# A cross-attention and mixture-of-experts layer on one core: the steps around the routing in a new order, pauses at every third scatter, and expert scatters sent singly at first

## The chip, the cores and the metric

The kernel runs on one core of a Trainium2 chip. Its time is the device time of one execution in microseconds (us); the runs shown are given by their median. A profile is one further execution, recorded by the hardware profiler, with its span in the same unit. Engines are called PE (TensorE), DVE (VectorE), ACT (ScalarE), POOL (GpSimd) and SP (SyncE).

## What is computed

`x` is 16 blocks of 128 tokens with 128 features, `ctx` has the same shape. The reference, cut to what matters:

```
def xattn(Q, K, V):                       # Q = layernorm(x), K = V = ctx, 16 heads of 8 features each
    Q_ = Q.reshape(B, L, 16, 8) @ Wq + bq # and K_, V_ in the same way, 64 wide
    scores = einsum('blhk,blgk->blhg', Q_, K_) / sqrt(64)   # per token: heads against heads
    y = einsum('blhg,blgv->blhv', softmax(scores), V_)
    return y.reshape(B, L, 1024) @ Wo + bo

def ffn(x):                               # 8 experts, top 2 of them per token, 2048 tokens
    probs = softmax(x @ router_w)
    expert_gate, expert_index = top_k(probs, 2)
    v = x @ (wv * sv)[e]
    y = gelu(x @ (w * s)[e])
    out = (v * y) @ (w1 * s1)[e]          # for both chosen experts e
    return sum(expert_gate * out)

x = x + xattn(layernorm(x), ctx, ctx)
x = x + ffn(layernorm(x))
```

## The kernel before

Everything is written out by hand: each engine has a program of its own, and semaphores join them. There are two stages that overlap in the middle.

**Attention.** 16 tiles of 128 tokens (NT = 16) go through a software pipeline in groups of four (G = 4, four groups NG, numbered 0 to 3). The `step(g, j)` of an engine issues what that engine does in one step for several tiles at once: `tile_at(g, j, lag)` gives the tile that is `lag` stages behind. The steps of the loop `STEADY` end with tile 15 entering the scores; what is left is written out behind the loop, engine by engine ("the end" below). For a tile t:

- ACT writes the first layernorm `xn` (L600), PE turns it (L844) and multiplies.
- DVE forms the products `qk` (L1114, 128x2048), PE sums them (L856), ACT copies `scoresT` (L610), PE finishes the scores (L865, L878).
- DVE: `maximum` (L1146, L1150); ACT: `exponentials` (L669); DVE: `normalise` (L1164 to L1168), which leaves `probs`.
- `values` (L318) multiplies probabilities with the context for a range of the 16 keys: POOL does the first 11 (`POOL_KEYS`) and DVE, as `value_share`, the last 5. For the last tile, 15, POOL does 6 (`LAST_POOL_KEYS`) and DVE 10. PE sums the products in `value_sum` (L899), ACT copies `zT` (`z_turned`, L650), PE makes the output in `output_sum` (L907 to L909), ACT copies it to `x_sb` (`residual`, L655).

**Routing.** When the four tiles of a group n are through, the group is normalised a second time and routed. DVE: `second_statistics` of each tile (L1174, L1177). POOL: `second_rstd` (L493 to L499), four small operations. ACT: `normed` (L678), four activations. PE: `second_turn` (L916); ACT: `turned` (L685); PE: `router_product` (L926). DVE: `choices` (L1187 to L1203), PE: `places` (L936 to L939), ACT: `logits_exponentials` (L701), DVE: `positions` (L1213 to L1228), ACT: `rows_but_gates` (L695, L696) and `gates_in` (L661). Then POOL scatters the group's rows to `routed` in DRAM with eight indirect DMAs of 128 rows (`scatters`, L540). Groups 0 and 1 send theirs without any wait, in portions that `sends(n)` lays between the steps of the loop. Groups 2 and 3 wait before every even scatter but the first until all earlier ones of the group have landed:

```
for m in range(first, end):
    if n >= EARLY_G and m and m % 2 == 0:
        pool.wait_ge(scattered[n], 16 * m)
    pool.indirect_dma_start(
```

The last group is split: `second_rstd` and `normed` are called for its first three tiles and then for the fourth. ACT's exponential and its GELU need different tables; `load_gelu` (L590) loads the latter early, and L701 carries a load of the former where it stands behind a GELU.

**Expert tiles.** The routed rows, sorted by expert, are 39 tiles of 128 rows (TILES = 39), numbered 0 to 38. Tiles 0 to 8 (EARLY = 9) hold rows of groups 0 and 1 alone and may start when these have landed; tiles 9 to 38 wait for all four groups. SP loads a tile into one of 12 buffers `xs` (XB = 12, L389), PE turns it (`turn_rows`, L961), ACT copies `xsT` (`rows_turned`, L718) and the gate weights `g_tile` (`gate_weights`, L713), DVE the value weights `v_tile` (L1308); PE does `products` (L976), ACT `gelu` (L725), DVE `hidden` (L1316), PE `down` (L995), DVE `gated` (L1325), which writes `yo`. POOL scatters `yo` to `expert_out` with one indirect DMA per tile (L561); before every even tile it waits until the scatter of the tile before has landed. SP loads tile t + 12 only when `y_sent` says that the scatter of tile t has landed, since it takes its buffer. `turn_rows` of a tile stands on PE ahead of `products` of the tile before it. Every engine takes its program in order; PE's `products(1, 1)` waits for `residual` of attention tile 15 (`x2_ready`), whose bank it uses.

**The last part.** When every expert scatter has landed (SP, L420), SP gathers `expert_out` in five pieces (L424), DVE adds the pairs and the residual (L1378, L1381), and SP stores (L427).

## Time and profile before

| | |
|---|---|
| median of 3 runs | 280.63 us (280.06 to 281.09) |
| the profiled execution | 278.34 us |
| its span | 276.6 us |
| PE busy | 237.7 us (86% of the span) |
| DVE busy | 178.0 us (64%) |
| POOL busy | 151.9 us (55%) |
| ACT busy | 118.5 us (43%) |
| TensorE clock granted | 0.952 of full speed over the span |

The profiled execution lies 1.74 us above its span (what is around it) and 2.29 us below the median. Times of the trace count from the start of the span. The attention takes about the first 136 us, expert tiles run from there to 260 us, and the gather, the sums and the store take the rest. The profile gives, for each instruction, its start, its duration, and how long its engine had been idle before it with what ended that idle time; and it gives the chain of waits, which is the path of work followed back from the last instruction.

### The profile page before, as it was taken

The page shows a single profiled execution, that of the slowest core. Times are in us where ns is not written, and L with a number is a line of the kernel's source. Part 1 is how long each engine was busy: PE and PEld are TensorE (multiplying, and loading weights), DVE is VectorE, ACT ScalarE, POOL GpSimd, SP SyncE. Part 2 cuts the span into 40 slices and gives each one's busy share as a digit, 9 for nine tenths or more (in the row PEclk, how much of TensorE's full clock was granted, in tenths as well). Part 3 has the DMA queues.
Part 4 walks back from the last instruction along what each step waited for, and adds up shares of the span by engine and source line. Part 5 has one row for each costly group of instructions (what it writes and reads, how often), then busy time and mean ns, then how long its engine had stood idle before and what let it go on. Part 6 is the DMA issues. An engine that isn't in the chain of part 4 may idle for free.

```text
span 276.6 us, 6414 instructions
## 1 busy us (share of the span) xinstructions
PE 237.7 (86%) x1883; PEld 223.0 (81%) x1884; DVE 178.0 (64%) x475; ACT 118.5 (43%) x297; POOL 151.9 (55%) x160
## 2 busy tenths in 40 slices
PE   7997999979997999797996985999999999999500
PEld 7976888868886888696896974999999999999400
DVE  2799799877998789969174472454465455555216
ACT  2443422464544563326485242454465555554000
POOL 6956549754688859886545555253532423333300
PEclk9999999999999999979899899899999999999955
DMA  5979999995000100001200112312221121000058
GB/s 143 301 186 419 294 315 382 378 380 197 1 19 17 34 11 22 29 31 40 59 31 29 49 32 67 79 57 52 59 58 34 53 55 39 28 10 26 3 181 274
DMA packets 25518, 30.94 MB, mean 112 GB/s; under 512 B 2652, under 2 KB 16896, under 8 KB 25362
## 3 DMA queue, kind: packets, MB, share of 16 engines
q1 hardware_dynamic: 21708, 25.28, 29.1%
q0 software_dynamic: 2528, 4.77, 5.5%
q10 hardware_dynamic: 1254, 0.55, 0.7%
q8 instruction: 14, 0.23, 0.3%
q14 instruction: 14, 0.11, 0.1%
HBM read 16.26 MB, written 14.79 MB: 112 GB/s over the span
## 4 chain that ended last, share of the span: by engine, by line
PE 63%; DVE 11%; DMA 10%; POOL 5%; issue 5%; ACT 4%; SPq 1%; POOLq 0%; ACTq 0%; DVEq 0%
PE bank L976 20%; PE bank L995 10%; PE bank L899 9%; PE bank L856 8%; DMA routed<-rows,pos 6%; DVE qk L1114 3%; PE bank L783 3%; POOL routed L540 3%; DMA pv<-expert_out 2%; POOL pv L318 2%; PE bank L865 2%; ACT xn L600 2%; PE bank L907 2%; PE bank L909 2%; PE bank L908 2%
## 5 line engine op out<-in xcount | busy, mean ns | idle before, releaser
L561 POOL DMA_INDIRECT expert_out<-yo,xs x39 | 38.1, 978 | 59.1 <-DVE yo L1325 36.3
L318 POOL TENSOR_TENSOR pv<-probs,ctx_sb 128x1408 f32<-128x1408 f32 (+1 forms) x16 | 45.9, 2868 | 21.8 <-DVE probs L1168 18.9
L1316 DVE TENSOR_TENSOR hid<-bank,act_sb 128x512 f32<-128x512 f32 x39 | 26.9, 690 | 30.7 <-PE bank L976 16.0
L540 POOL DMA_INDIRECT routed<-rows,pos x32 | 35.0, 1093 | 21.1 <-DMA routed<-rows,pos 9.8
L995 PE MATMUL bank<-w_sb,hid 128*128 x312 | 43.1, 283 | 2.5 <-DVE yo L1325 2.4
L976 PE MATMUL bank<-xsT,g_tile 128*128 128x128 f32 x312 | 42.6, 280 | 1.1 <-issue 1.1
L995 PEld LDWEIGHTS bank<-w_sb,hid 128*128 128x128 f32 x312 | 39.4, 198 | 3.1 <-issue 3.1
L976 PE MATMUL bank<-xsT,v_tile 128*128 128x128 f32 x312 | 41.8, 277 | 0.0
L976 PEld LDWEIGHTS bank<-xsT,g_tile 128*128 128x128 f32 x312 | 39.1, 197 | 1.4 <-issue 1.3
L976 PEld LDWEIGHTS bank<-xsT,v_tile 128*128 128x128 f32 x312 | 38.5, 194 | 0.0
L1114 DVE TENSOR_TENSOR qk<-bank,ctx_ig 128x2048 f32<-128x2048 f32 x16 | 36.5, 2285 | 2.3 <-ACT ctx_ig L585 1.9
L856 PE MATMUL bank<-ident,qk 128*128 128x128 f32 x256 | 32.1, 281 | 2.6 <-DVE qk L1114 2.6
L899 PE MATMUL bank<-ident,pv 128*128 128x128 f32 x256 | 32.2, 281 | 1.6 <-POOL pv L318 1.6
L725 ACT ACTIVATE act_sb<-bank 128x512 f32<-128x512 f32 x39 | 23.3, 597 | 22.6 <-PE bank L976 19.8
L899 PEld LDWEIGHTS bank<-ident,pv 128*128 128x128 f32 x256 | 30.2, 146 | 3.3 <-issue 2.2
L713 ACT COPY g_tile<-g_sb 128x512 f32 x39 | 24.1, 618 | 19.0 <-PE bank L976 14.7
L856 PEld LDWEIGHTS bank<-ident,qk 128*128 128x128 f32 x256 | 29.6, 145 | 3.0 <-issue 3.0
L1308 DVE COPY v_tile<-v_sb 128x512 f32 x39 | 17.1, 438 | 18.2 <-issue 16.9
L1325 DVE SCALAR_TENSOR_TENSOR yo<-bank,xs,wo_sb 128x128 f32<-128x128 f32 x39 | 13.7, 351 | 11.2 <-PE bank L995 8.8
L318 DVE TENSOR_TENSOR pv<-probs,ctx_sb 128x640 f32<-128x640 f32 (+1 forms) x16 | 20.4, 1276 | 0.1
L718 ACT COPY xsT<-bank 128x128 f32<-128x128 f32 x39 | 10.3, 264 | 17.5 <-PE bank L961 17.3
L610 ACT COPY scoresT<-bank 128x256 f32<-128x256 f32 x16 | 6.0, 373 | 27.2 <-PE bank L856 24.3
(171 smaller groups left out, 330.0 us busy)
## 6 DMA issues: line engine op xcount, KB each, us to landing
routed<-pad_rows SPq DMA_DIRECT2D x4, 2080.0 KB, 20.5
xs<-routed SPq DMA_DIRECT2D x39, 65.0 KB
g_sb<-in_L_ffn_w_dram SPq DMA_DIRECT2D x1, 2048.0 KB, 11.7
g_scale<-in_L_ffn_s_dram SPq DMA_DIRECT2D x1, 2048.0 KB, 16.3
v_sb<-in_L_ffn_wv_dram SPq DMA_DIRECT2D x1, 2048.0 KB, 28.0
pv<-expert_out SPq DMA_DIRECT2D x3, 512.0 KB, 4.9
x_sb<-in_x_dram SPq DMA_DIRECT2D x4, 256.0 KB, 6.2
ctx_sb<-in_ctx_dram SPq DMA_DIRECT2D x4, 256.0 KB, 6.3
```

The lines of the kernel that those rows point to most:

```text
L318: return eng.tensor_tensor(pv[:, b, g0:g1, :, :], probs[:, b, :, g0:g1].rearrange("p h g -> p g h").unsqueeze(3).to_broadcast([P, many, H, ...
L540: pool.indirect_dma_start(out=routed[:, :], out_offset=bass.IndirectOffsetOnAxis(ap=pos[:, m % TOP, m // TOP:m // TOP + 1], axis=0), in_=r ...
L561: pool.indirect_dma_start(out=expert_out[:, :], out_offset=bass.IndirectOffsetOnAxis(ap=xs_i[:, t % XB, P:P + 1], axis=0), in_=yo[:, t % X ...
L713: nc.scalar.copy(g_tile[:, c % 2, :], g_sb[:, bass.ds(at, F)]).then_inc(g_tile_ready, 1)
L725: nc.scalar.activation(act_sb[:, c % 2, :], bank[1 + c % 2][:, :], ACT.Gelu_apprx_tanh).then_inc(act_ready, 1)
L856: mm = nc.tensor.matmul(part, qk[:, b, i, c * P:(c + 1) * P], ident[:, :], start=(i == 0), stop=(i == HD - 1), is_transpose=True)
L899: mm = nc.tensor.matmul(bank[4][:, 0:P], pv[:, t % 2, key, :, :].rearrange("p h i -> p (h i)"), ident[:, :], start=(key == 0), stop=(key = ...
L976: mm = nc.tensor.matmul(psum[:, n * P:n * P + P], weights[:, c % 2, n * P:n * P + P], xsT[:, c % 2, :], start=True, stop=True)
L995: mm = nc.tensor.matmul(y_bank(t, c)[:, 0:P], hid[:, c % 2, n * P:n * P + P], w1_sb[:, bass.ds(y_at + n * P, P)], start=(n == 0), stop=(n ...
L1114: v.tensor_tensor(qk[:, b, :, :].rearrange("p i (h g) -> p i h g", h=H), q_bank(b)[:, 0:P].rearrange("p (i h) -> p i h", i=HD).unsqueeze(3 ...
L1308: v.tensor_copy(v_tile[:, c % 2, :], v_sb[:, bass.ds(at, F)]).then_inc(v_tile_ready, 1)
L1316: v.tensor_tensor(hid[:, c % 2, :], bank[3 + c % 2][:, :], act_sb[:, c % 2, :], ALU.mult).then_inc(hid_ready, 1)
```

## The change

Seven edits, by engine:

1. POOL, in the loop: `second_rstd` of a group stands behind `values` of its step, no longer ahead of it.
2. ACT, in the loop: `normed` moves from the end of a step into the next step, behind the exponentials and ahead of the copy of `scoresT`.
3. POOL: group 1 sends 3, 3 and 2 scatters between steps instead of 2, 3 and 3; groups 2 and 3 wait before every third scatter instead of every second; and a wait for all eight scatters of the group is added behind each of these groups.
4. POOL and DVE, at the end: POOL has no part of the values of tile 15, DVE does all 16 keys. POOL sends four scatters of group 2, not one, ahead of the last group's `second_rstd`.
5. POOL: expert scatters 1 to 11 wait each for the one before; scatters from 12 on wait for none.
6. ACT, PE, DVE, at the end: routing steps of group 2 go ahead of steps of tile 15 (`choices`, `places`, `logits_exponentials`, `gates_in`), `products(0, 0)` goes ahead of `value_sum(15)`, `normed` of the last group's first three tiles goes ahead of `residual(15)`, and `second_statistics(15)` goes behind `hidden(0, 0)`, the weights of tile 2 and `left_table`.
7. ACT: `gelu(2, 2)` goes ahead of the exponentials of the last group and of the two table loads.

```diff
-            return {9: 3, 10: 6, 11: G * TOP} if n < EARLY_G - 1 else {8: 2, 9: 5, 10: G * TOP}
+            return {9: 3, 10: 6, 11: G * TOP} if n < EARLY_G - 1 else {8: 3, 9: 6, 10: G * TOP}
...
+        IN_A_ROW = 3
@@ POOL, step @@
-                    if a := group_at(g, j, NORM):
-                        second_rstd(a[0])
                     a = tile_at(g, j, 1)
...
                         values(pool, t, b, 0, POOL_KEYS).then_inc(pv_pool, 1)
+                    if a := group_at(g, j, NORM):
+                        second_rstd(a[0])
@@ POOL, scatters @@
-                        if n >= EARLY_G and m and m % 2 == 0:
+                        if n >= EARLY_G and m and m % IN_A_ROW == 0:
                             pool.wait_ge(scattered[n], 16 * m)
@@ POOL, the end @@
-                pool.wait_ge(p_normed, NT)
-                pool.wait_ge(zT_psum, NT - 2)
-                values(pool, NT - 1, (NT - 1) % 2, 0, LAST_POOL_KEYS).then_inc(pv_pool, 1)
-                scatters(NG - 2, 0, 1)
+                scatters(NG - 2, 0, 4)
                 second_rstd(NG - 1, 0, G - 1, NG)
                 second_rstd(NG - 1, G - 1, G, NG + 1)
-                scatters(NG - 2, 1, G * TOP)
+                scatters(NG - 2, 4, G * TOP)
+                pool.wait_ge(scattered[NG - 2], SENT)
                 scatters(NG - 1, 0, G * TOP)
+                pool.wait_ge(scattered[NG - 1], SENT)

                 for t in range(TILES):
                     pool.wait_ge(yo_ready, t + 1)
-                    if t and t % 2 == 0:
-                        pool.wait_ge(y_sent[(t - 1) % XB], 16 * ((t - 1) // XB + 1))
+                    if 0 < t < XB:
+                        pool.wait_ge(y_sent[t - 1], 16)
@@ ACT, step @@
                     if a := tile_at(g, j, 1):
                         exponentials(a[0])
+                    if a := group_at(g, j, LOGITS):
+                        normed(a[0])
...
-                    if a := group_at(g, j, NORM):
-                        normed(a[0])
@@ PE, value_sum @@
-                    pe.wait_ge(pv_pool, t + 1)
+                    if t < NT - 1:
+                        pe.wait_ge(pv_pool, t + 1)
@@ ACT, the end @@
-                exponentials(NT - 1)
                 logits_exponentials(NG - 2)
                 gate_weights(0, 0)
+                exponentials(NT - 1)
                 z_turned(NT - 2)
                 rows_but_gates(NG - 2)
+                gates_in(NG - 2)
                 residual(NT - 2)
                 rows_turned(0, 0)
                 load_gelu()
-                gates_in(NG - 2)
+                gelu(0, 0)
+                gate_weights(1, 1)
                 z_turned(NT - 1)
-                gate_weights(1, 1)
+                rows_turned(1, 1)
+                normed(NG - 1, 0, G - 1, NG)
                 residual(NT - 1)
-                rows_turned(1, 1)
-                gelu(0, 0)
-                normed(NG - 1, 0, G - 1, NG)
-                normed(NG - 1, G - 1, G, NG + 1)
                 gate_weights(2, 2)
                 gelu(1, 1)
+                normed(NG - 1, G - 1, G, NG + 1)
+                turned(NG - 1)
                 rows_turned(2, 2)
-                turned(NG - 1)
                 gate_weights(3, 3)
+                rows_but_gates(NG - 1)
                 rows_turned(3, 3)
-                rows_but_gates(NG - 1)
+                gelu(2, 2)
                 logits_exponentials(NG - 1)
                 load_gelu()
-                gelu(2, 2)
                 gates_in(NG - 1)
@@ PE, the end @@
+                places(NG - 2)
                 value_sum(NT - 2)
-                places(NG - 2)
                 output_sum(NT - 2)
                 turn_rows(0, 0, 0)
+                products(0, 0)
                 value_sum(NT - 1)
                 turn_rows(1, 1, 0)
                 output_sum(NT - 1)
-                products(0, 0)
                 products(1, 1)
@@ DVE, the end @@
                 value_share(NT - 2)
                 value_weights(0, 0)
+                choices(NG - 2)
                 maximum(NT - 1)
-                choices(NG - 2)
                 normalise(NT - 1)
-                value_share(NT - 1, LAST_POOL_KEYS)
                 positions(NG - 2)
+                value_share(NT - 1, 0)
                 second_statistics(NT - 3)
                 second_statistics(NT - 2)
                 value_weights(1, 1)
-                second_statistics(NT - 1)
                 hidden(0, 0)
                 value_weights(2, 2)
                 left_table()
+                second_statistics(NT - 1)
                 hidden(1, 1)
```

Three places where instructions change their order. First POOL, from the step that normalises group 2 (`vtmp2` to `shift2`) to the end of the attention; `pv` are the values, `routed` the scatters.

```order
+L317 TENSOR_TENSOR pv<-probs,ctx_sb 128x1408
 L493 TENSOR_TENSOR vtmp2<-mv2,eps 128x4
 L495 TENSOR_TENSOR rstd2<-vtmp2,minus_half 128x4
 L496 TENSOR_TENSOR centre2<-mv2,minus_one 128x4
 L499 TENSOR_TENSOR shift2<-centre2,rstd2 128x4
-L318 TENSOR_TENSOR pv<-probs,ctx_sb 128x1408
-L540 DMA routed<-rows0,pos0 18432x130 x3
-L318 TENSOR_TENSOR pv<-probs,ctx_sb 128x1408
-L318 TENSOR_TENSOR pv<-probs,ctx_sb 128x768
-L540 DMA routed<-rows0,pos0 18432x130
+L540 DMA routed<-rows0,pos0 18432x130 x2
+L317 TENSOR_TENSOR pv<-probs,ctx_sb 128x1408
+L540 DMA routed<-rows0,pos0 18432x130 x4
```

The values of tile 13 now stand ahead of the four small operations, the 128x768 values of tile 15 are gone, and group 2's first four scatters stand together behind the values of tile 14.

Second ACT at the same place in the loop, from `z_turned` of tile 12: before,

```order
L650 COPY zT<-bank 128x128
L655 COPY x_sb<-bank 128x128
L678 ACTIVATE xn<-x_sb,shift,rstd 128x128 x4
L669 ACTIVATE probs<-shifted 128x256
L610 COPY scoresT<-bank 128x256
```

and with the change:

```order
L649 COPY zT<-bank 128x128
L654 COPY x_sb<-bank 128x128
L668 ACTIVATE probs<-shifted 128x256
L677 ACTIVATE xn<-x_sb,shift,rstd 128x128 x4
L611 COPY scoresT<-bank 128x256
```

The four activations of `normed` have moved behind the exponentials; in the steps of groups 0 and 1 the first layernorm's `xn` (L600) stands between the first two of these rows and the exponentials, so it is passed too.

Third ACT at the end, from `load_gelu` on. Before,

```order
L590 ACTIVATE pause_act<-eps 128x1
L661 COPY rows0<-gates0 128x8
L650 COPY zT<-bank4 128x128
L710 TENSOR_LOAD w_off
L710 ISA x2
L713 ISA
L713 COPY g_tile<-g_sb 128x512
L655 COPY x_sb<-bank4 128x128
L718 COPY xsT<-bank0 128x128
L725 ACTIVATE act_sb<-bank1 128x512
L678 ACTIVATE xn2<-x_sb,shift2,rstd2 128x128 x4
```

and with the change:

```order
L589 ACTIVATE pause_act<-eps 128x1
L724 ACTIVATE act_sb<-bank1 128x512
L709 TENSOR_LOAD w_off
L709 ISA x2
L712 ISA
L712 COPY g_tile<-g_sb 128x512
L649 COPY zT<-bank4 128x128
L717 COPY xsT<-bank0 128x128
L677 ACTIVATE xn2<-x_sb,shift2,rstd2 128x128 x3
L654 COPY x_sb<-bank4 128x128
```

The copy of the gates has left this stretch for a place ahead of the table load, and the copy of tile 15's output to `x_sb` stands behind three activations that need POOL's `shift2`.

## Rows read from the trace of the kernel before

**Rows 1.** Timeline, 55 to 58 us: ACT, then PE's next row. Start, duration, engine, instruction, [idle before].

```profile
55.56 1.65 ACT L678 ACTIVATE xn<-x_sb,shift,rstd 128x128 f32<-128x128 f32 x4
57.11 0.48 ACT L600 ACTIVATE xn<-x_sb,shift,rstd 128x128 f32<-128x128 f32 x1
...
57.64 0.33 PE L844 MATMUL bank<-ident,xn 128*128 128x128 f32 x1 [1.84 <-ACT xn L600]
```

**Rows 2.** Timeline, 78 to 88 us: DVE's share of the values twice, and POOL's.

```profile
78.51 0.81 DVE L318 TENSOR_TENSOR pv<-probs,ctx_sb 128x640 f32<-128x640 f32 x1
...
85.03 3.26 DVE L318 TENSOR_TENSOR pv<-probs,ctx_sb 128x640 f32<-128x640 f32 x1
...
84.77 2.84 POOL L318 TENSOR_TENSOR pv<-probs,ctx_sb 128x1408 f32<-128x1408 f32 x1
```

**Rows 3.** Timeline, 114 to 121 us: DVE's products of tile 15, and PE's sum of them.

```profile
114.38 2.29 DVE L1114 TENSOR_TENSOR qk<-bank,ctx_ig 128x2048 f32<-128x2048 f32 x1
...
116.81 3.44 PE L856 MATMUL bank<-ident,qk 128*128 128x128 f32 x16 [1.50 <-DVE qk L1114]
```

**Rows 4.** Timeline, 127 to 136 us: DVE, POOL and ACT, where the attention ends.

```profile
127.92 1.49 DVE L318 TENSOR_TENSOR pv<-probs,ctx_sb 128x1280 f32<-128x1280 f32 x1
...
127.97 2.94 POOL L318 TENSOR_TENSOR pv<-probs,ctx_sb 128x768 f32<-128x768 f32 x1 [2.26 <-DVE probs L1168]
132.87 1.02 POOL L540 DMA_INDIRECT routed<-rows,pos  x1 [1.96 <-ACT rows L661]
134.20 0.88 POOL L495 TENSOR_TENSOR rstd<-vtmp,minus_half 128x3 f32<-128x3 f32 x1
...
131.81 0.19 ACT L661 COPY rows<-gates 128x8 f32<-128x8 f32 x1
```

**Rows 5.** Timeline, POOL, 138 to 166 us: scatters 1 and 2 of group 2, then 0, 2 and 7 of group 3.

```profile
138.86 1.19 POOL L540 DMA_INDIRECT routed<-rows,pos  x1 [0.51 <-issue]
141.63 0.97 POOL L540 DMA_INDIRECT routed<-rows,pos  x1 [1.58 <-DMA routed<-rows,pos]
...
151.87 1.05 POOL L540 DMA_INDIRECT routed<-rows,pos  x1 [0.30 <-issue]
...
155.80 0.97 POOL L540 DMA_INDIRECT routed<-rows,pos  x1 [1.60 <-DMA routed<-rows,pos]
...
164.98 0.97 POOL L540 DMA_INDIRECT routed<-rows,pos  x1 [0.30 <-issue]
```

**Rows 6.** Timeline, ACT, 143 to 150 us: a table load, and the copy of the last group's gates.

```profile
145.32 1.28 ACT L590 ACT_TABLE_LOAD   x1
146.61 0.20 ACT L590 ACTIVATE pause_act<-eps 128x1 f32<-128x1 f32 x1
...
149.60 0.20 ACT L661 COPY rows<-gates 128x8 f32<-128x8 f32 x1 [2.30 <-DVE gates L1226]
```

**Rows 7.** Chain of waits, 164 to 175 us: start, duration, what.

```profile
164.98 2.39 DMA routed<-rows,pos
...
168.67 1.44 DMA xs<-routed
...
170.49 2.46 PE bank L976 x16
```

**Rows 8.** Timeline, PE: the turn of expert tile 9, and that of tile 23.

```profile
170.16 0.33 PE L961 MATMUL bank<-ident,xs 128*128 128x128 f32 x1 [3.33 <-DMA xs<-routed]
...
211.01 0.27 PE L961 MATMUL bank<-ident,xs 128*128 128x128 f32 x1
```

**Rows 9.** Timeline, POOL: expert scatters 2, 6 and 38; then DVE's last `yo`.

```profile
170.59 0.97 POOL L561 DMA_INDIRECT expert_out<-yo,xs  x1 [2.10 <-DMA expert_out<-yo,xs]
...
180.50 0.97 POOL L561 DMA_INDIRECT expert_out<-yo,xs  x1 [3.30 <-DMA expert_out<-yo,xs]
...
262.26 0.97 POOL L561 DMA_INDIRECT expert_out<-yo,xs  x1 [2.05 <-DMA expert_out<-yo,xs]
...
259.74 0.35 DVE L1325 SCALAR_TENSOR_TENSOR yo<-bank,xs,wo_sb 128x128 f32<-128x128 f32 x1 [0.77 <-PE bank L995]
```

1 line of the change is left out of this document (removed).

## The prediction

> **What bounds the kernel now.** I read the chain of waits first, then the timeline of each engine where the chain changes hands. Up to 107 us the chain runs on PE, with short pieces of ACT. At the boundary of a group it carries an extra piece: ACT does the four activations of `normed` from 55.56 to 57.11 us, only then the `xn` of the next tile, and PE has been idle for 1.84 us when that arrives [rows 1]; it recurs at 86 us. Then DVE takes over: PE waits 1.50 us for `qk` of tile 15 [rows 3]. At the end of the attention the chain goes through POOL's values of tile 15, which run beside DVE's and end at 130.9 us; POOL's scatter 0 of group 2 starts at 132.87, behind ACT's copy of the gates [rows 4]. From 138.86 to 164.98 us the chain is POOL and the landing of its scatters [rows 5]; the last one lands after 2.39 us, SP loads expert tile 9 at 168.67 [rows 7], and PE, idle for 3.33 us, goes on at 170.16 [rows 8]. From there PE runs at 2.79 us per expert tile until 258.5 us. So what counts is when PE can turn tile 9, and what follows the last `yo`: scatter 38 waits until 262.26 us, though its input was done at 260.09 [rows 9].
>
> **The change, part by part.** Edit by edit, in the order of time.
>
> *`normed` behind `xn` (edits 1 and 2).* At group 0 `xn` starts 57.11 - 55.56 = 1.55 us earlier [rows 1]. `normed` then runs beside PE's sum over `qk`, and POOL's `shift2` is ready for it although `values` now precedes it. At group 1 POOL has three scatters ahead of both, so `shift2` comes after another 2.84 us of values [rows 2]; I lay `normed` out to end some 0.7 us after PE wants its results for `second_turn`. Gain 1.55 + 0.85 = 2.4 us. Bounds for the two together: 0.6 us (both late) and 3.1 us (none).
>
> *Three scatters of group 1 instead of two (edit 3).* The third puts POOL's values of tile 12 back by 1.27 us (0.97 + 0.30) [rows 5]. DVE's share takes 0.81 us alone and 3.26 us where it starts 0.26 us behind POOL's 2.84 us: it gets done only when POOL is through [rows 2]. The share of tile 12 meets POOL's values, so DVE, which by then sets the pace [rows 3], loses some 1.2 us. Bounds: nothing (it had slack) and 2.45 us, the whole of 3.26 - 0.81. The Trainium skill, "GPSIMD Engine Reference", Key points, says that GpSimd shares its SBUF interfaces with VectorE, contention being with VectorE instructions in a 2-port mode or with two SBUF inputs. The trace agrees, and the same rule speaks for edit 4, where DVE's last share runs with POOL idle. Left after these: 1.2 us at tile 15.
>
> *The end of the attention (edits 4 and 6).* With `choices(2)` ahead of `maximum(15)` and `places(2)` ahead of `value_sum(14)`, DVE finishes `positions(2)` near 128.1 us. ACT copies the gates ahead of the table load at 128.85, 2.95 us earlier than at 131.81, so scatter 0 of group 2 moves from 132.87 to 129.9 [rows 4]. DVE's 16 keys cost 2.29 us, the row of the same size [rows 3], and end at 130.4 us, before PE wants them. POOL then goes scatters 0 to 3: 1.27 + 1.27 + 2.57 (0.97 and a wait of 1.60) + 0.97 = 6.1, to 136.0 [rows 5]; `second_rstd` of three tiles some 1.7 us around its 0.88 us power [rows 4], to 137.7. Here is the **new wait**: ACT stands at `normed` of these tiles with `residual(15)` behind it. `normed` takes 1.25 us (three quarters of 1.65 [rows 1]), `residual` and DVE's statistics 0.85, POOL's last `second_rstd` 1.35: done at 141.2 us instead of 138.35 (138.86 less 0.51 [rows 5]), 2.85 us later. PE's `products(1, 1)` wait for the same residual until 139.3, idle for over 4 us, and go on at a lower clock; PE has about 4 us to spare before tile 9, so this costs nothing as long as that lasts.
>
> *Group 2's last scatters and the last group's routing (edits 3, 6, 7).* Scatters 4 to 7 start at 141.7, 143.0, 145.5 and 146.8; with the added wait for all eight, POOL is free at 149.4. The routing of group 3 begins 2.85 us late, but `gelu(2, 2)` no longer stands behind two table loads of 1.28 us each [rows 6], so that `hidden(2, 2)` and `positions(3)` follow at once. I get the exponentials' end at 148.7, `positions` at 149.9 and, behind the GELU table load, the gates at 150.2, against 149.60 [rows 6]. The first scatter of group 3 then starts 1.06 us after the copy, as at group 2 [rows 4]: 151.25, against 151.87 [rows 5], so 0.6 us earlier. Bounds: 149.4 (POOL alone, 2.45 us earlier) and 153.9 (150.2 + 1.06 and another 2.6 us, one turn of a waited scatter).
>
> *Every third instead of every second.* From scatter 0 to 7 of group 3 it is 164.98 - 151.87 = 13.1 us now, with three waits [rows 5]. With two waits it is 5 x 1.27 + 2 x 2.6 = 11.6 us. That holds if three in flight land as fast as two; scatters behind another one land no later than single ones (2.39 us [rows 7]), so I take the full 1.5 us; bounds 0 and 1.5. The last scatter starts at 162.9 instead of 165.0, and tile 9 is turned 2.1 us earlier, near 168.1.
>
> *Expert scatters (edit 5).* A waited one takes 0.97 + 2.10 = 3.07 us [rows 9]. The first can go when group 3 has landed, at 165.5; scatters 1 to 11 in single file put scatter 11 at 165.5 + 11 x 3.07 = 199.3, and with one long one of 4.27 us (0.97 + 3.30 [rows 9]) at 200.5. Its landing (2.7) and SP's load (2.7, from 167.4 to 170.1 [rows 7, 8]) make tile 23 ready at 205.9. PE turns tile 23 at 211.01 now [rows 8] and at 208.9 with the gain: 3 us to spare. Behind scatter 11 POOL sends one each 1.27 us and has caught up by tile 24 or so. Cost nothing; when the cover is gone PE waits one for one. At the tail the wait of scatter 38 goes: it starts 1.27 us behind scatter 37, which goes at 259.24, so at 260.5 instead of 262.26. Gain 1.75 us.
>
> **Sum.** -2.1 (tile 9) - 1.75 (tail) = -3.85 us. The profiled execution would go from 278.34 to 274.5; it lies 2.3 us below the median of 280.63, so I forecast 276.8 us for the median. What a measurement here can tell from no change is 0.5%, 1.4 us. The forecast case spans -5.6 to -2.
>
> **Rivals.**
> - *The routing of the last group eats the scatters' gain* (15 in 100). For it: the new wait on ACT, and PE running slow behind its idle time: 16 transposes took 3.44 us after 1.50 us idle [rows 3], and `products` 2.46 after 3.33 us [rows 7]. Against it: 0.6 us of room on that path before it is even with now, and 1.5 from the waits behind it. With 2.1 us more delay only the tail is left: 280.63 - 1.75 = 278.9; with 3.5 more, 280.3.
> - *Slower: the buffers starve* (10 in 100). The place is expert scatters 1 to 11. Now a pair takes 1.27 + 3.07, or 2.17 us per tile, under PE's 2.79; single file takes 3.07, above it. It decides where the mean of the eleven passes 3.07 + (4.2 / 11) = 3.45 us, which uses up the room. If all were of the long kind, 4.27 us, they would take 11 x 1.2 = 13.2 us more, less 4.2 of room: PE loses 9.0 us, and the kernel takes 276.8 + 9.0 = 285.8 us. For it: long waits exist [rows 9]. Against it: most are near 3.07.
> - *More than forecast* (7 in 100). `gates_in` of group 3 in time for POOL alone, 149.4: another 1.85 us, 275.0.
> - *Table loads cost twice what their row says* (3 in 100). Then the last gates come behind two further stretches of 1.3 us: the gain at tile 9 is gone, with 0.5 us lost, and the tail leaves 279.4. Against it: 1.28 us load from 145.32, and the next activation starts at 146.61 [rows 6]. The Trainium skill, "ScalarE: Activation LUTs", What ACT_TABLE_LOAD costs, gives about 1.28 us for the load and about 1.38 for a drain, 2.66 in all; the row shows the first alone.
> - *The change does nothing* is within the first: the waits and the order are on the engines' queues as written.
>
> **How the numbers follow.** Forecast case 65, rivals 15, 10, 7 and 3 in 100. Faster by over 0.5% (under 279.2): 65 + 7 and half of the first rival, 0.79. Within 0.5%: the rest of it and the fourth, 0.11. Slower: 0.10. The range reaches from the third rival, with some of the front bounds, at 274.4, to the first and fourth, at 279.8; the slower rival is left outside.
>
> **What would show it right or wrong.** In the new profile: no ACT `xn` behind four activations at 55 and 86 us, tile 15's `qk` about 1 us earlier; group 2's first scatter near 130; ACT idle before `normed` until 137.7 and PE idle before tile 1's products over 4 us; eight scatters of group 3 in 11.6 us from 151.2; tile 9 turned near 168.1; expert scatters 3.07 us apart until 200 us and no PE wait for a load between 180 and 212; last scatter at the last `yo`. Wrong it would be if tile 9 is turned after 170, if three scatters in a row land later, or if PE waits for `xs` anywhere behind tile 9.

## The result, and the profile after

The changed kernel took 281.43 us (median of 4 runs, 281.18 to 283.07), beside 280.86 us (4 runs) for the kernel before in the same session. The ratio is 1.0138, with a 95% interval of 1.0077 to 1.0198. The same kernel run again on another chip (c_after, below) gave 1.0022 [0.9965, 1.0079]. The medians alone differ by 0.2%; a ratio compares only executions in the faster of the two states in which one kernel is found, so that here and below it need not equal the quotient of the medians. So the change is level to somewhat slower, and not the 1.4% faster of the forecast. Its profiled execution took 281.27 us.

The page of the changed kernel: span, busy time, granted clock in 40 slices of 7 us, and the chain by engine.

```profile
span 279.4 us, 6405 instructions
PE 240.2 (86%) x1883; PEld 223.7 (80%) x1884; DVE 183.6 (66%) x475; ACT 119.4 (43%) x297; POOL 148.9 (53%) x159
PEclk9999999999999999868589998799999999999965
PE 49%; DVE 18%; issue 10%; POOL 9%; DMA 8%; ACT 3%; SPq 1%; DVEq 1%; POOLq 0%; ACTq 0%
```

The same clock line of the kernel before:

```profile
PEclk9999999999999999979899899899999999999955
```

DVE is busy 5.6 us longer than before (183.6 against 178.0) with the same number of instructions; 0.8 us of that is work taken over from POOL (tile 15's values take 2.29 us instead of 1.49), the rest is instructions that take longer. The clock falls deeper and longer between 112 and 147 us, down to 0.5 of full speed in one slice. The timeline of the changed kernel, 112 to 127 us (start, duration, engine, instruction, [idle before and what ended it]), says where DVE's time went:

```profile
112.35 3.46 DVE L1247 TENSOR_SCALAR w_off<-tile_e 128x9 int32<-128x9 f32 x1
112.92 2.84 POOL L317 TENSOR_TENSOR pv<-probs,ctx_sb 128x1408 f32<-128x1408 f32 x1
116.66 2.29 DVE L1114 TENSOR_TENSOR qk<-bank,ctx_ig 128x2048 f32<-128x2048 f32 x1
119.10 3.65 PE L855 MATMUL bank<-ident,qk 128*128 128x128 f32 x16 [5.88 <-DVE qk L1114]
122.03 3.50 POOL L317 TENSOR_TENSOR pv<-probs,ctx_sb 128x1408 f32<-128x1408 f32 x1 [1.63 <-DVE probs L1168]
123.00 2.82 DVE L1308 COPY v_tile<-v_sb 128x512 f32 x1 [0.19 <-issue]
```

In the kernel before, the timeline of DVE has for the first of these:

```profile
113.12 0.17 DVE L1247 TENSOR_SCALAR w_off<-tile_e 128x9 int32<-128x9 f32 x1
```

An instruction on nine numbers per partition takes 3.46 us instead of 0.17: it ends at 115.81, just when POOL's values of tile 13 end (112.92 + 2.84 = 115.76). Then `qk` of tile 15, which was to come 1.2 us sooner than before, ends 2.3 us later, and PE waits 5.88 us for it instead of 1.50 [rows 3]. Its 16 matmuls then run at half the clock (3.65 us; 1.91 at full clock, for the tile before). They did so before the change too, for the most part (3.44 us [rows 3]). The copy of `v_tile` (0.43 us where POOL computes nothing) is held for 2.82 us in the same way.

The timeline of the changed kernel again, from the end of the attention to the last output: ACT, then POOL, PE and DVE.

```profile
134.12 0.20 ACT L660 COPY rows<-gates 128x8 f32<-128x8 f32 x1
...
143.21 1.26 ACT L677 ACTIVATE xn<-x_sb,shift,rstd 128x128 f32<-128x128 f32 x3 [0.38 <-POOL shift L499]
144.38 0.24 ACT L654 COPY x_sb<-bank 128x128 f32<-128x128 f32 x1
```

```profile
135.20 1.02 POOL L540 DMA_INDIRECT routed<-rows,pos  x1 [9.67 <-ACT rows L660]
...
156.45 0.97 POOL L540 DMA_INDIRECT routed<-rows,pos  x1 [1.67 <-DMA routed<-rows,pos]
...
162.58 0.97 POOL L540 DMA_INDIRECT routed<-rows,pos  x1 [2.61 <-DMA routed<-rows,pos]
...
168.96 0.97 POOL L540 DMA_INDIRECT routed<-rows,pos  x1 [0.30 <-issue]
...
265.04 0.97 POOL L560 DMA_INDIRECT expert_out<-yo,xs  x1 [0.30 <-DVE yo L1325]
```

```profile
174.28 0.48 PE L961 MATMUL bank<-ident,xs 128*128 128x128 f32 x1 [4.61 <-DMA xs<-routed]
...
215.54 0.27 PE L961 MATMUL bank<-ident,xs 128*128 128x128 f32 x1
...
264.33 0.35 DVE L1325 SCALAR_TENSOR_TENSOR yo<-bank,xs,wo_sb 128x128 f32<-128x128 f32 x1 [0.83 <-PE bank L995]
```

Against [rows 4, 5, 8, 9] the two profiles differ, stretch by stretch, by this much (after minus before). The milestones are the starts of the first `second_turn`, of the copy of group 2's gates, of the scatters, and of PE's turns of tiles 9 and 38, and the end of `qk` of tile 15 at 118.95 and 116.67 us:

| stretch | measured | forecast |
|---|---|---|
| start to `second_turn` of group 0 (57.45, 59.55) | -2.10 | -1.55 |
| to the end of `qk` of tile 15 | +4.38 | +0.35 |
| to the copy of group 2's gates | +0.03 | -1.75 |
| to the first scatter of group 3 | +2.27 | +2.35 |
| to its last scatter | -0.60 | -1.5 |
| to tile 9 turned | +0.14 | 0 |
| tile 9 to tile 38 (257.38, 252.84) | +0.42 | 0 |
| tile 38 to the last instruction | -1.75 | -1.75 |
| sum | +2.79 | -3.85 |

Of the difference of 6.6 us between sum and forecast, 4.0 us lie in one stretch, the one with the held `w_off` (3.29 us of it), and 1.8 in the next, in which the copy of `v_tile` is held.

### The profile page after: what moved, and what is told of

It reads as the page before. It is cut to its first block, busy times and chain, and to the rows that moved or that the text cites. A ratio compares the mean times of both kernels' runs of the same rounds, so it can differ in the third digit from the quotient of the medians.

```text
span 279.4 us, 6405 instructions
## 1 busy us (share of the span) xinstructions
PE 240.2 (86%) x1883; PEld 223.7 (80%) x1884; DVE 183.6 (66%) x475; ACT 119.4 (43%) x297; POOL 148.9 (53%) x159
## 4 chain that ended last, share of the span: by engine, by line
PE 49%; DVE 18%; issue 10%; POOL 9%; DMA 8%; ACT 3%; SPq 1%; DVEq 1%; POOLq 0%; ACTq 0%
PE bank L976 22%; PE bank L995 11%; PE bank L899 4%; POOL routed L540 4%; DVE qk L1114 4%; PE bank L855 4%; DMA routed<-rows,pos 3%; DVE pv L317 2%; DMA x_sb<-in_x_dram 2%; POOL pv L317 2%; DMA pv<-expert_out 2%; PE bank L961 1%; DVE w_off L1247 1%; DVE v_tile L1308 1%; ACT xn L599 1%
## 5 line engine op out<-in xcount | busy, mean ns | idle before, releaser
L317 POOL TENSOR_TENSOR pv<-probs,ctx_sb 128x1408 f32<-128x1408 f32 x15 | 43.6, 2907 | 20.3 <-DVE probs L1168 17.5
L540 POOL DMA_INDIRECT routed<-rows,pos x32 | 33.3, 1041 | 30.4 <-ACT rows L660 12.2
L976 PE MATMUL bank<-xsT,g_tile 128*128 128x128 f32 x312 | 43.4, 284 | 2.4 <-issue 1.1
L976 PE MATMUL bank<-xsT,v_tile 128*128 128x128 f32 x312 | 42.9, 282 | 0.0
L995 PE MATMUL bank<-w_sb,hid 128*128 x312 | 42.0, 278 | 0.2 <-DVE hid L1316 0.2
L976 PEld LDWEIGHTS bank<-xsT,v_tile 128*128 128x128 f32 x312 | 39.7, 199 | 0.0
L995 PEld LDWEIGHTS bank<-w_sb,hid 128*128 128x128 f32 x312 | 38.5, 194 | 0.7 <-issue 0.5
L1308 DVE COPY v_tile<-v_sb 128x512 f32 x39 | 20.0, 512 | 18.0 <-issue 17.7
L1325 DVE SCALAR_TENSOR_TENSOR yo<-bank,xs,wo_sb 128x128 f32<-128x128 f32 x39 | 13.7, 351 | 12.8 <-PE bank L995 11.4
L317 DVE TENSOR_TENSOR pv<-probs,ctx_sb 128x640 f32<-128x640 f32 (+1 forms) x16 | 18.9, 1184 | 0.0
## 6 DMA issues: line engine op xcount, KB each, us to landing
g_scale<-in_L_ffn_s_dram SPq DMA_DIRECT2D x1, 2048.0 KB, 15.3
```

The lines of the kernel that those rows point to most:

```text
L317: return eng.tensor_tensor(pv[:, b, g0:g1, :, :], probs[:, b, :, g0:g1].rearrange("p h g -> p g h").unsqueeze(3).to_broadcast([P, many, H, ...
L540: pool.indirect_dma_start(out=routed[:, :], out_offset=bass.IndirectOffsetOnAxis(ap=pos[:, m % TOP, m // TOP:m // TOP + 1], axis=0), in_=r ...
L976: mm = nc.tensor.matmul(psum[:, n * P:n * P + P], weights[:, c % 2, n * P:n * P + P], xsT[:, c % 2, :], start=True, stop=True)
L995: mm = nc.tensor.matmul(y_bank(t, c)[:, 0:P], hid[:, c % 2, n * P:n * P + P], w1_sb[:, bass.ds(y_at + n * P, P)], start=(n == 0), stop=(n ...
L1308: v.tensor_copy(v_tile[:, c % 2, :], v_sb[:, bass.ds(at, F)]).then_inc(v_tile_ready, 1)
```

## The experiments

The theory after the result (A): edit 1 puts POOL's values of tile 13 beside DVE's early expert table (a dozen small operations, `w_off` and `row_off` among them, that work out which expert each of the first nine tiles belongs to), and some of DVE's instructions stand until POOL is through. Rivals: the lower clock after a wait (C), the new order of the end (B), the single expert scatters (edit 5).

**Four kernels made from the change.** Line numbers shift by one or two in them.

a_wait_table: POOL's values of tile 13 wait for the table.

```diff
+                        if t == NT - 3:
+                            pool.wait_ge(early_ready, 1)
                         values(pool, t, b, 0, POOL_KEYS).then_inc(pv_pool, 1)
```

> The changed kernel, with one wait more: POOL's values of attention tile 13 wait until DVE has finished the early table. Theory A (a DVE instruction of the table, w_off at L1247, is held while POOL's values run: 3.46 us for a 128x9 operation that took 0.17 before the change): the row goes back to 0.17, qk of tile 15 ends 3.3 us earlier (near 115.6 instead of 118.95), PE's idle time before it falls from 5.9 to about 2.6 us, and the kernel takes about 4 us less than the changed one, near 277. Theory B (the long row is an effect of something else, and the loss comes from ACT standing at normed with tile 15's residual behind it): L1247 or the instructions behind it stay as long, and the time stays within 1 us of the changed kernel's 281.4.

a_rstd_first: edit 1 undone, `second_rstd` ahead of `values` in POOL's step.

```diff
+                    if a := group_at(g, j, NORM):
+                        second_rstd(a[0])
                     a = tile_at(g, j, 1)
...
-                    if a := group_at(g, j, NORM):
-                        second_rstd(a[0])
```

> The changed kernel with edit 1 alone undone: second_rstd stands ahead of POOL's values in its step again, so that the values of tile 13 start about 1.9 us later, near 114.8, behind the early table (which without a hold ends at 113.3). Theory A: L1247 takes 0.17 us, qk of tile 15 ends 3.3 us earlier, the hold moves to DVE's share of tile 13 (1.7 us for 0.8), and the time is 3 to 4 us under the changed kernel's. Theory B: no change beyond 1 us.

a_table_late: DVE builds the table behind `qk` of tile 15.

```diff
+                    if g * G + j == EARLY_TABLE + 2:
+                        early_table()
...
-                        early_table()
```

> The changed kernel with DVE's early table (12 small operations, about 3 us without a hold) behind qk of tile 15 instead of ahead of it. Theory A: qk of tile 15 ends at about 113, 6 us earlier (3.3 of hold and about 2.7 of the table's own time), PE waits for it hardly at all; the table itself then follows beside POOL's second_rstd and scatters and is not held, or costs 2 us of slack there. Time 5 to 6 us under the changed kernel's, near 276. Theory B: at most the table's own 2.7 us are won.

a_warm: PE does 24 filling matmuls before it waits for `qk` of tile 15.

```diff
+                        if t == NT - 1:
+                            fill(24)
                         pe.wait_ge(qk_ready, t + 1)
```

> The changed kernel with 24 products of the identity in front of PE's wait for qk of tile 15, which fill most of its 5.9 us of idle time; nothing else moves. This measures what the lower granted clock costs by itself (granted clock 0.67 in the stretch from 120 to 140). If the clock is a cost on the path: L855 of tile 15 takes 1.9 us instead of 3.65, the value sums of tiles 14 and 15 1.9 instead of 2.7, group 2's first scatter comes 2 us or more earlier, and the time falls by 2 to 3 us. If it is not: the granted clock rises, and the time stays within 0.7 us of 281.4.

Ratios to the kernel before: a_wait_table 1.0004 [0.9945, 1.0062], a_rstd_first 0.9997 [0.9944, 1.0050], a_table_late 1.0052 [1.0010, 1.0095], a_warm 1.0039 [0.9981, 1.0097]. The first three were each expected 3 to 6 us below the change's 281.4 us; their medians are 280.15, 278.36 and 280.20, that of the kernel before, run beside them, 279.90. The change itself was not run beside them. DVE's timeline of a_wait_table, then of a_rstd_first:

```profile
113.38 0.17 DVE L1249 TENSOR_SCALAR w_off<-tile_e 128x9 int32<-128x9 f32 x1
...
120.90 0.50 DVE L1310 COPY v_tile<-v_sb 128x512 f32 x1 [0.19 <-issue]
```

```profile
112.12 0.17 DVE L1247 TENSOR_SCALAR w_off<-tile_e 128x9 int32<-128x9 f32 x1
...
120.64 2.98 DVE L1308 COPY v_tile<-v_sb 128x512 f32 x1 [0.19 <-issue]
```

With POOL elsewhere the instruction is short again, and the stretch from the first `second_turn` to the end of `qk` of tile 15 falls from 61.5 us in the change to 58.4 and 57.4 (57.1 before). In the five profiles of kernels that have edit 1, and the table where it was, `w_off` takes 3.45 or 3.46 us (the change, c_after, a_warm, b_12, e_after_pairs); in the other thirteen it takes 0.17 or 0.18. So the hold, and edit 1 as its cause in this place, is shown. What it costs the whole kernel is not: both kernels only come level with the one before, and the change's own two ratios are 1.0138 and 1.0022, so that taking the hold out gave between 1.4% and nothing clear of noise.

In a_table_late `qk` of tile 15 ends earliest of all, 55.7 us after the first `second_turn`, and still nothing is gained. Its table meets POOL's values in the new place too (POOL's start at 114.47 and take 2.85 us), the copy of `v_tile` is held for 2.81 us, and the copy of group 2's gates comes 18.4 us behind `qk`, against 15.2 in the change. DVE's timeline of a_table_late:

```profile
114.57 0.21 DVE L1269 TENSOR_REDUCE n_tiles<-over 128x8 f32<-128x64 f32 x1
114.81 2.54 DVE L1270 TENSOR_SCALAR jump<-n_tiles 128x8 f32<-128x8 f32 x1
```

Of two small neighbours that both read and write SBUF, the reduction is not held and the TENSOR_SCALAR is.

In a_warm the matmuls run at full clock, and little comes of it, since DVE is held as before: the gates of group 2 come 14.8 us behind `qk` instead of 15.2. PE's timeline of a_warm:

```profile
119.86 1.97 PE L857 MATMUL bank<-ident,qk 128*128 128x128 f32 x16 [0.48 <-DVE qk L1116]
```

So the clock is worth at most 0.4 us here (C falls for this place), although PE itself needs 1.7 us less.

**The change again, and its halves.** c_after is the change itself. b_end keeps its end of the attention alone (edits 4, 6 and 7, and from edit 3 the pauses at every third scatter and the waits for all eight; edits 1, 2, 5 and the third scatter of group 1 undone). b_normed is the kernel before with edit 2 alone. d1 is b_normed with pauses at every third scatter, `gelu(2, 2)` ahead of the exponentials (edit 7), and no wait for expert scatters from tile 12 on.

```diff
# b_normed: ACT's step of the kernel before
                         exponentials(a[0])
+                    if a := group_at(g, j, LOGITS):
+                        normed(a[0])
...
-                    if a := group_at(g, j, NORM):
-                        normed(a[0])
# d1, on top of it
-                        if n >= EARLY_G and m and m % 2 == 0:
+                        if n >= EARLY_G and m and m % 3 == 0:
...
+                gelu(2, 2)
                 logits_exponentials(NG - 1)
                 load_gelu()
-                gelu(2, 2)
...
-                    if t and t % 2 == 0:
-                        pool.wait_ge(y_sent[(t - 1) % XB], 16 * ((t - 1) // XB + 1))
+                    if 0 < t < XB and t % 2 == 0:
+                        pool.wait_ge(y_sent[t - 1], 16)
```

> The changed kernel as it is, once more, as a control: run on the same chip and in the same rounds as the three beside it. Theory A and B both expect the trace of the first one: w_off at L1247 about 3.5 us, PE idle 5 to 6 us before the sum over qk of tile 15, and a time 0 to 1.5% above the kernel before.

> The loop of the kernel before (edits 1, 2, the order of group 1's scatters and edit 5 undone) with the end of the change: its new order on ACT, PE and DVE, tile 15's values on DVE alone, four scatters of group 2 first, waits at every third and behind each group. Theory A2 (beside the held instruction, the new end costs time itself: ACT stands at normed with tile 15's residual behind it, so the last group's shift2 comes late): counted from the first second_turn, the last shift2 comes 6 to 8 us later than in the kernel before (78.8 us there), the first scatter of group 3 2 to 3 us later, the turn of expert tile 9 1 to 1.5 us later; time 1 us over the kernel before. My prediction's theory (the new end is no loss, because the routing of the last group catches up): tile 9 is turned 2 us earlier than before.

> The kernel before with edit 2 alone: ACT's normed stands behind the exponentials of the next step, POOL's second_rstd stays ahead of the values. Expected if that edit is sound: the first two group boundaries are 1.5 us shorter each, POOL's values of tile 13 stay behind DVE's early table (both move by the same 3 us), no instruction of the table is held, and the kernel takes 2.5 to 3 us less than before, 277.5 where the kernel before takes 280.5. If the gain at the boundaries is always given back on DVE, whatever POOL does (the rival): qk of tile 15 ends where it did, within 0.7 us.

> The kernel before with edit 2, scatters of groups 2 and 3 waiting at every third (without the waits added behind each group), gelu(2, 2) ahead of the two table loads (edit 7), expert scatters in pairs up to tile 11 and without a wait from tile 12 on; POOL's order in the loop and the end of the attention stay as before. Theory A and A2: 3 us from the boundaries, 1.2 from group 2's scatters and 1.3 from group 3's, 1.75 at the tail: 6 to 7 us less than the kernel before, near 274. If the waits behind each group are needed for speed (scatters piling up land later), the 2.5 us of the scatters are missing: 276.5.

c_after 1.0022 [0.9965, 1.0079], b_end 1.0029 [0.9967, 1.0091], b_normed 0.9868 [0.9773, 0.9962], d1 0.9757 [0.9635, 0.9879]. Edit 2 alone is thus worth 1.3%, with an interval from 0.4 to 2.3%, about as much as the forecast gave the whole change (1.4%). Its profiled execution was one of its longest (279.97 us; median 278.30) and shows the gain only up to the end of `qk` of tile 15, 2.0 us earlier than before. The new end without the rest gains nothing: in b_end's profile (283.49 us, its longest execution) the first scatter of group 2 comes 14.9 us behind `qk` of tile 15 (16.2 before, 1.3 sooner), but the last shift of group 3 ends 26.9 us behind it (21.7 before). ACT's timeline of b_end:

```profile
145.22 1.26 ACT L677 ACTIVATE xn<-x_sb,shift,rstd 128x128 f32<-128x128 f32 x3 [4.38 <-POOL shift L499]
146.39 0.24 ACT L654 COPY x_sb<-bank 128x128 f32<-128x128 f32 x1
```

That is the wait of the forecast, ACT at `normed` behind POOL's four scatters with `residual(15)` behind it, and it costs 5.2 us at this point; the forecast laid out 2.85, which from tile 15's earlier end is 4.05. In d1, with the old end of the attention, the eight scatters of group 3 take 11.5 us (151.63 to 163.17), as forecast (11.6).

**Edit 1 by itself, a fill, the holds, and no pause.** b_12 is b_normed with edit 1. b_fill is the kernel before with 8 filling matmuls instead of one at each group's boundary. a_no_holds is a_rstd_first with `value_weights(0, 0)` behind `choices(2)` and `maximum(15)`, away from POOL's values. d2 is d1 without any pause in the scatters of groups 2 and 3.

```diff
# b_12: POOL's step, on top of b_normed
-                    if a := group_at(g, j, NORM):
-                        second_rstd(a[0])
...
                         values(pool, t, b, 0, POOL_KEYS).then_inc(pv_pool, 1)
+                    if a := group_at(g, j, NORM):
+                        second_rstd(a[0])
# b_fill
-                            fill(1)
+                            fill(8 if group_at(g, j, LOGITS) else 1)
# a_no_holds: DVE, on top of a_rstd_first
-                value_weights(0, 0)
                 choices(NG - 2)
                 maximum(NT - 1)
+                value_weights(0, 0)
# d2, on top of d1
-                        if n >= EARLY_G and m and m % 3 == 0:
-                            pool.wait_ge(scattered[n], 16 * m)
```

> The kernel before with edits 1 and 2: normed behind the exponentials and POOL's second_rstd behind the values. It differs from the run with edit 2 alone by POOL's order only. Theory A (a DVE instruction beside POOL's values is held): POOL's values of tile 13 start right behind its scatters, beside DVE's early table; one row of the table (w_off, s_off or jumps) takes 2.5 to 3.5 us instead of 0.2, qk of tile 15 ends 2.5 to 3 us later than with edit 2 alone (56.3 us behind the first second_turn there), and the 1.3% that edit 2 alone won is lost again. Without that mechanism the two are equal within 0.7 us.

> The kernel before with seven more products of the identity in PE's idle time of 1.84 us at the first two group boundaries; nothing else. Theory C: this idle time lies where the granted clock sometimes falls (in the profile of the run with the new end alone the sum over qk behind it took 3.62 us, in the profile of before 1.91), which is why runs of the kernel before spread from 277 to 282 us. Then these runs gather at the lower end, median 1 to 2 us under before, and the spread shrinks. If the clock has no part in the spread: median and spread as before, within 0.5 us.

> The changed kernel with second_rstd ahead of the values again (as the earlier run) and DVE's value weights of expert tile 0 behind choices and maximum, so that neither the early table nor that copy meets POOL's values. Theory A: the copy takes 0.43 us instead of 2.98, and group 2's first scatter starts 15 us behind the end of qk of tile 15 instead of 17.7; what is left of the loss is the new end's own (the last shift2 5 us later than before): time 2.5 to 4 us under before. If holds were not what mattered: as the run with second_rstd moved alone, level with before.

> The version with edit 2, edit 7 and no wait at the tail (d1), now with no wait at all between the scatters of groups 2 and 3. It tells whether scatters in a long row land later. If they do not: group 3's scatters take 7 x 1.27 = 8.9 us instead of 11.5, its first one comes at the gates, 1 to 2 us earlier, tile 9 is turned 3 to 4 us earlier unless PE itself arrives there first (it had 2.5 to 3 us to spare), and the kernel takes 2 to 3 us less than d1, 1.03 times faster than before or more. If they do: the last landing is more than 4 us behind the last issue, and the time is that of d1 within 1 us.

b_12 1.0035 [0.9984, 1.0086]: with edit 1 the gain of b_normed is not there. The two differ by POOL's order alone, but were run in different sessions; their intervals do not overlap. In the profiles the stretch from the first `second_turn` to the end of `qk` of tile 15 is 60.3 us against 56.3, and 3.3 us of that is the hold. DVE's and PE's timeline of b_12, then of b_normed:

```profile
111.94 3.46 DVE L1247 TENSOR_SCALAR w_off<-tile_e 128x9 int32<-128x9 f32 x1
...
118.69 3.65 PE L856 MATMUL bank<-ident,qk 128*128 128x128 f32 x16 [4.63 <-DVE qk L1114]
```

```profile
111.20 0.18 DVE L1247 TENSOR_SCALAR w_off<-tile_e 128x9 int32<-128x9 f32 x1
...
114.83 1.94 PE L856 MATMUL bank<-ident,qk 128*128 128x128 f32 x16 [1.25 <-DVE qk L1114]
```

b_fill 1.0103 [1.0027, 1.0179]: a miss. It was to keep PE's clock up at the boundaries and made the kernel slower; why is not shown. d2 1.0078 [1.0028, 1.0128]: a miss too, expected 2 to 3 us below d1. In its profile DVE is held again, by another instruction of the same table:

```profile
113.32 2.75 DVE L1270 SCALAR_TENSOR_TENSOR row_off<-tile_no,tile_row 128x9 int32<-128x9 f32 x1
```

and ACT stops twice: for 4.5 us until 147.87, in a row of seven scatters with no wait (140.62 to 148.50), and from 158.6 us for 7.6 us, in a row of ten (155.40 to 166.91). ACT's timeline of d2 ("remote" is a releaser that is none of the kernel's engines or transfers in view):

```profile
157.94 0.62 ACT L711 COPY g_tile<-g_sb 128x512 f32 x1
166.18 0.27 ACT L716 COPY xsT<-bank 128x128 f32<-128x128 f32 x1 [7.61 <-remote]
```

a_no_holds 1.0191 [1.0086, 1.0296], the greatest miss: `qk` of tile 15 ends at 115.1 us and the first scatter of group 2 starts at 130.95, 4.3 us ahead of the change, and yet the kernel is 1.9% slower. ACT's timeline of a_no_holds has the same stop, while POOL issues nine expert scatters in a row, 205.51 to 215.71:

```profile
207.70 0.62 ACT L712 COPY g_tile<-g_sb 128x512 f32 x1 [0.68 <-PE bank L976]
215.57 0.27 ACT L717 COPY xsT<-bank 128x128 f32<-128x128 f32 x1 [7.25 <-remote]
```

The turn of the tile had been on PE at 208.01, and so ACT had its input from 208.3 on. DVE stops as well, for 5.91 us until 214.23.

**Edit 5 by itself.** Four kernels follow up the stop of a_no_holds: e_nh_pairs and e_after_pairs are a_no_holds and the change with edit 5 undone, e_b_single is the kernel before with edit 5, e_d1_pairs is d1 with the waits of before between expert scatters.

```diff
# e_b_single; the other three have the lines of before here
-                    if t and t % 2 == 0:
-                        pool.wait_ge(y_sent[(t - 1) % XB], 16 * ((t - 1) // XB + 1))
+                    if 0 < t < XB:
+                        pool.wait_ge(y_sent[t - 1], 16)
```

> The run of the change without holds was 1.9% slower than before although the attention's end came early: in its trace ACT and DVE stand from 208 to 214-216 us while POOL issues nine expert scatters in a row with no wait between them (205.5 to 216.7), and PE loses some 5 us. Here the same kernel gets the waits of before between pairs of expert scatters (edit 5 undone, nothing else). If the long unwaited row is the cause: no idle time of over 2 us on ACT between 175 and 262 us, the ratio at 0.98 to 0.99. Rival, the loss has another cause (the chip, the clock): the ratio stays at 1.01 to 1.02.

> The change with edit 5 alone undone (waits between pairs of expert scatters as before). Theory, edit 5 costs on average some time by the stall behind unwaited scatters in some executions: 1 to 2 us faster than the change, ratio to before 0.995 to 1.000, and less scatter between executions. Rival, edit 5 gains (the tail's 1.75 us came from it): ratio 0.5% above the change's control at 1.002.

> The kernel before with edit 5 alone (each of the first expert scatters waits for the one ahead of it, those behind for none). By the prediction's term: the last outputs 1.75 us sooner, ratio 0.994. By the theory of the stall: a row of some ten unwaited scatters about 205 to 220 us, in some executions 3 to 7 us lost on ACT and DVE, ratio 1.00 to 1.01.

> The fastest kernel so far (norm early, thirds of the scatters, gelu ahead of the table) with every pair of expert scatters waiting as before. If rows of unwaited scatters cost: as fast as or faster than 0.976; if dropping the later waits gained: 0.5% slower, 0.981.

All in one session: e_b_single **1.0203 [1.0148, 1.0258]**, e_nh_pairs 0.9907 [0.9850, 0.9963], e_after_pairs 1.0136 [1.0090, 1.0182], e_d1_pairs 0.9767 [0.9709, 0.9825] (272.44 us beside 280.15). ACT, PE and POOL in the timeline of e_b_single, 203 to 217 us:

```profile
204.02 0.62 ACT L713 COPY g_tile<-g_sb 128x512 f32 x1 [0.37 <-PE bank L976]
...
209.79 0.27 ACT L718 COPY xsT<-bank 128x128 f32<-128x128 f32 x1 [5.16 <-remote]
...
214.15 0.60 ACT L725 ACTIVATE act_sb<-bank 128x512 f32<-128x512 f32 x1 [4.09 <-remote]
```

```profile
204.63 0.27 PE L961 MATMUL bank<-ident,xs 128*128 128x128 f32 x1
...
210.11 0.40 PE L961 MATMUL bank<-ident,xs 128*128 128x128 f32 x1 [2.53 <-issue]
210.36 2.05 PE L976 MATMUL bank<-xsT,g_tile 128*128 128x128 f32 x8
```

```profile
203.86 0.97 POOL L561 DMA_INDIRECT expert_out<-yo,xs  x1 [0.30 <-issue]
...
211.53 0.97 POOL L561 DMA_INDIRECT expert_out<-yo,xs  x1 [0.30 <-issue]
```

ACT stands twice, 9.3 us in all, in and just behind the row of scatters 11 to 18 (202.58 to 211.53 us); the stretch from tile 9's turn to tile 23's takes 46.3 us, against 40.9 before [rows 8]: 5.5 us lost. The tail from tile 38's turn is 19.76 us, 1.75 less than the 21.51 before, exactly the forecast's term. With 0.8 us lost up to tile 9 that makes the 4.55 us by which this profile ends later. With the waits back (e_nh_pairs) no such stop is in the trace, and the ratio is 2.8% lower than that of a_no_holds, taken in another session.

So edit 5 by itself costs time; that is shown. That the row of unwaited scatters is what stops ACT is not: it is argued from where the stops lie, and three things don't fit. The change has a row of twelve (207.99 to 222.08 us) with no stop in its profile, and so have a_wait_table, a_rstd_first, a_table_late and a_warm; c_after has one of thirteen (209.45 to 224.88). Undoing edit 5 in the change was expected to gain 1 to 2 us and gained nothing (e_after_pairs 1.0136). And ACT stopped in shorter rows too: in d2's of seven, and for 4.6 us until 153.16 in one of five in e_d1_pairs, the fastest kernel of all. d1, whose longest row is five, is as fast as e_d1_pairs. What is shown is that ACT stopped, for 4 to 8 us at a time, in the three profiles with rows of eight, nine and ten, and in none of the six with twelve or thirteen. What it waits for is not shown.

## Why the prediction was wrong

- **`normed` behind `xn`, gain 2.4 us (edits 1 and 2)**: the mechanism was right and edit 2 delivers it. PE's idle time of 1.84 us is 0.30 in the changed kernel, at both boundaries, and `second_turn` of group 1 starts 2.9 us earlier (86.95 against 89.85), 0.6 us of which was there from the first tiles on. But the two edits were costed together, and edit 1 only as a delay of `shift2`. This is **the step that failed**, the term for edit 1's effect on DVE, which was put at nothing: of the step that is moved, POOL's values of tile 13, the forecast asked who waits for it, and not which of DVE's instructions now run beside it. `w_off` was held 3.29 us longer on the path that sets the pace, and the stretch up to `qk` of tile 15 cost 4.38 us where 0.35 was forecast. With edit 1 undone that stretch is 4.1 us shorter (a_rstd_first, 57.4 against 61.5). In the whole time, b_normed gains 1.3% and b_12, with edit 1 on top, nothing. The stretch accounts for 4.0 of the 6.6 us between forecast and profile; that undoing edit 1 in the change brings back that much of its whole time is not shown.
- **DVE loses 1.2 us at tile 12 (edit 3)**: the hold was looked for in the one kind of instruction for which the rows showed it, those of L318 with two inputs in SBUF [rows 2], and there it took place (2.71 us at 106.55, against 1.39 before: 1.3 us, the size forecast). The Trainium skill, "GPSIMD Engine Reference", Specifications, names two kinds: instructions with two SBUF inputs and those in a 2-port mode. The first kind was priced, the second not. The instructions held in the change have one SBUF tensor as input (`w_off`, and the copy of `v_tile`); whether they ran in such a mode no row shows.
- **Scatter 0 of group 2 at 129.9 (edits 4 and 6)**: it came at 135.20, 3.5 us late through tile 15 and 1.8 us later than forecast behind it. From the end of `qk` of tile 15 to the copy of the gates 13.4 us were forecast. It took 15.2 in the change, 13.6 in e_nh_pairs and 14.7 in a_no_holds, both with the copy out of POOL's way, but also 15.3 in a_wait_table, where the copy of `v_tile` took only 0.50 us. So the term was right to 2 us, and the held copy is not shown to be what made up the rest.
- **ACT stands at `normed`: this costs nothing as long as PE's 4 us last**: too cheap, by all that the runs show. Against e_d1_pairs, in the same session and with the old end, e_nh_pairs is 1.4% slower. The two differ in more than this wait (the third scatter of group 1, the waits behind each group, the place of one copy on DVE), and the profiled execution of e_nh_pairs was its longest (280.40 us; median 278.30), so the share of the wait is argued. ACT's timelines of the two, e_nh_pairs first:

```profile
139.94 1.26 ACT L677 ACTIVATE xn<-x_sb,shift,rstd 128x128 f32<-128x128 f32 x3 [3.47 <-POOL shift L499]
141.11 0.24 ACT L654 COPY x_sb<-bank 128x128 f32<-128x128 f32 x1
```

```profile
133.34 0.27 ACT L655 COPY x_sb<-bank 128x128 f32<-128x128 f32 x1 [0.42 <-PE bank L909]
...
134.95 1.27 ACT L678 ACTIVATE xn<-x_sb,shift,rstd 128x128 f32<-128x128 f32 x3
```

  The residual of tile 15 comes 7.8 us later, 2.4 of it because tile 15 was late by as much (the stretch before it, with the third scatter of group 1, is 57.7 us against 55.9). The routing of the last group goes with it: its first scatter starts at 153.25 us instead of 148.36, although group 2's was earlier (131.37, 132.20). The last group is on the path to tile 9; group 2 is not, once POOL has time to spare between them (3.16 us idle before 153.25).
- **Every third: 11.6 us**: 12.5 in the change (156.45 to 168.96), 11.5 in d1, 11.8 in e_d1_pairs, 13.7 in e_nh_pairs, where one wait took 3.68 us. Right, with the size uncertain by 2 us.
- **"Cost nothing" for edit 5**: in the change's profile it held. Scatter 11 went at 207.99, 7.5 us later than forecast (6.3 of it by the late start of scatter 0, 171.82, the rest by a mean period of 3.29 us instead of 3.18), PE never waited for `xs` behind tile 9, and the tail gained 1.75 us. The rival in which the buffers starve fell. But the term was not safe: by itself on the kernel before, edit 5 costs 2.0% instead of gaining 0.6%, and in its profile 5.5 us are lost between the turns of tiles 9 and 23, where the forecast took the row of unwaited scatters for free. A small misreading had no effect: PE's 2.79 us per expert tile hold from tile 23 on; from tile 9 to 23 it is 2.92 [rows 8].
- **The rivals**: the one ending slower had the wrong mechanism (no tile waited for a buffer). The first, "the routing eats the gain", names the place of a part of it.

## What to carry to other kernels

Before a long elementwise instruction is moved on POOL, write down which DVE instructions it will then run beside, and look in the traces at hand which kinds are held until POOL is through, however small they are. Here these were, beside POOL's values, the products of two SBUF tensors (`pv`, and `row_off` in d2), the TENSOR_SCALARs `w_off` and `jump`, and the copy of `v_tile`. Reductions from SBUF were not (`n_tiles`, 0.21 us in a_table_late; `picked`, 0.22 us from 93.02 in d1, with POOL's values from 91.36), nor was `qk`, which reads PSUM (2.29 us from 113.11 in d1, with POOL's values from 114.24). Cost edits one by one: b_normed, one move of two lines, gives 1.3%, and e_d1_pairs (edits 2 and 7 and the pauses at every third scatter) 2.3% over the kernel before, both hidden in a change that came out level. And a wait between transfers that seems to cost 2 us is not free to drop: test it alone, as e_b_single does.

## What the hardware showed that was not expected

- A DVE instruction on 128x9 elements takes 0.17 us alone and up to 3.46 us beside POOL's values of 2.84; its row starts 0.57 us ahead of POOL's (112.35 and 112.92) and ends with POOL's. Its neighbours of the same size, before and after, are short, so that some 0.5 us of timing decide whether one is hit: in d2 it was `row_off`, in a_table_late `jump`. It can go the other way: DVE's share of tile 14, 0.05 us ahead of POOL's values (121.98 and 122.03), took its usual 0.82 us, and POOL's took 3.50 instead of 2.84.
- In or just behind rows of unwaited indirect scatters, one each 1.27 us, ACT stopped for 7.25 us (a_no_holds), 7.61 us (d2) and 5.16 plus 4.09 us (e_b_single). It is open what it waits for, and why six profiles with longer rows, the change's own among them, had no such stop.
- The median of the kernel before was between 278.94 and 281.01 us over the five sessions, and the change's own ratio was 1.0138 in one and 1.0022 in another, their intervals just overlapping. A difference under 1% in one session was no proof here.
